# A four-layer graph network on one core: the step grid cut from 100 to 98 blocks of 32 destinations, and the dense layers' chunks from six of 512 and one of 128 to five of 512, one of 320 and one of 256

## What is computed

```python
h = relu(layernorm(x)); x = x + L0(h)   # messages relu([h[src],h[dst],ea]@mW1+mb1)@mW2, mean over dst, update, norm
h = relu(layernorm(x)); x = x + h @ W1 + b1 + segment_sum(h[src], dst) @ W2 + b2
h = relu(layernorm(x)); x = x + segment_sum(norm[:, None] * (h @ W)[src], dst) + bias
h = relu(layernorm(x)); x = x + relu(0.9 * segment_sum(h[src] * norm[:, None], dst) + 0.1 * h)
```

## Time and profile before

| what | value |
|---|---|
| device time, median of 3 runs | 948.86 us (948.36 to 949.64) |
| span of the profiled execution, first to last instruction | 946.8 us |
| PE busy | 851.2 us, 90% of the span |
| DVE, ACT, POOL busy | 67%, 54%, 55% |
| mean granted TensorE clock | 0.957 of full speed |

### The profile page before, as it was taken

How to read it: one execution, slowest core, us unless ns; L and a number is a source line. 1 busy time by engine, 2 the same in 40 slices (tenths; PEclk the granted TensorE clock), 3 DMA queues, 4 the chain that set the end, 5 groups by cost and what they waited for, 6 DMA issues and landing times.

```text
span 946.8 us, 19062 instructions
## 1 busy us (share of the span) xinstructions
PE 851.2 (90%) x6997; PEld 788.9 (83%) x6997; DVE 636.1 (67%) x1758; ACT 510.7 (54%) x1013; POOL 520.9 (55%) x496
## 2 busy tenths in 40 slices
PE   3257889889898978999989999999999999999997
PEld 2257879879898978989989999987889888888886
DVE  6528979887786877779897989968743311115664
ACT  2224757556575656768777788853353011114873
POOL 5477777777777777777777777745110000023110
PEclk9667999999898989999999999999999999999999
DMA  8752556556565666556565556656247778784500
GB/s 206 199 109 71 159 160 209 165 159 214 174 200 158 173 142 192 165 165 204 168 184 156 176 159 196 176 172 195 70 157 274 295 297 299 297 287 139 165 23 27
DMA packets 109503, 168.91 MB, mean 178 GB/s; under 512 B 14723, under 2 KB 69545, under 8 KB 109406
## 3 DMA queue, kind: packets, MB, share of 16 engines
q1 hardware_dynamic: 92062, 137.01, 44.8%
q0 software_dynamic: 13648, 28.21, 11.5%
q10 hardware_dynamic: 3696, 2.42, 0.9%
HBM read 109.15 MB, written 58.44 MB: 177 GB/s over the span
## 4 chain that ended last, share of the span: by engine, by line
PE 43%; POOL 38%; issue 13%; DMA 4%; ACT 1%; SPq 1%; DVE 1%; ACTq 0%; POOLq 0%; DVEq 0%
POOL room L769 36%; PE ps L1889 14%; PE ps L1874 14%; PE ps L1714 2%; DMA room<-p_rows,idx 2%; PE ps L1715 2%; PE ps L1728 2%; PE ps L1858 2%; PE ps L1745 2%; PE ps L1747 2%; PE ps L1650 1%; DMA w_m<-in_L_gnn_mW 1%; POOL pair L769 1%; DMA p_rows<-g 1%; ACTq L905 0%
## 5 line engine op out<-in xcount | busy, mean ns | idle before, releaser
L769 POOL DMA_INDIRECT room<-p_rows,idx x416 | 438.0, 1053 | 137.5 <-issue 125.0
L1714 PE MATMUL ps<-room,ident 128*128 128x128 f32 x832 | 178.8, 299 | 59.7 <-DMA room<-p_rows,idx 58.9
L1714 PEld LDWEIGHTS ps<-room,ident 128*128 128x128 f32 x832 | 135.5, 205 | 63.5 <-DMA room<-p_rows,idx 45.6
L1715 PE MATMUL ps<-room 128*128 128x128 f32 x832 | 170.6, 289 | 0.0
L1745 PE MATMUL ps<-room 128*128 128x200 bf16 x800 | 161.3, 253 | 0.0
L1747 PE MATMUL ps<-room 128*128 128x100 bf16 x1600 | 160.6, 208 | 0.0
L1294 DVE TENSOR_TENSOR room<-room,Wp 128x800 bf16<-128x800 bf16 x300 | 155.4, 571 | 0.0
L1747 PEld LDWEIGHTS ps<-room 128*128 128x128 bf16 x1600 | 147.9, 98 | 3.9
L1889 PE MATMUL ps<-room,h 128*128 128x256 f32 (+1 forms) x650 | 136.2, 371 | 0.0
L1715 PEld LDWEIGHTS ps<-room 128*128 128x128 f32 x832 | 136.0, 205 | 0.0
L927 ACT ACTIVATE g<-ps 128x512 f32<-128x512 f32 x104 | 62.2, 598 | 136.8 <-PE ps L1715 136.7
(11 more groups left out here) (195 smaller groups left out, 1132.1 us busy)
## 6 DMA issues: line engine op xcount, KB each, us to landing
weight_blocks<-room SPq DMA_DIRECT2D x50, 800.0 KB, 4.6
room<-weight_blocks SPq DMA_DIRECT2D x12, 3200.0 KB
room<-dst_row SPq DMA_DIRECT2D x52, 256.0 KB
room<-count_blocks SPq DMA_DIRECT2D x8, 1600.0 KB
count_blocks<-room SPq DMA_DIRECT2D x50, 200.0 KB
room<-p_rows,idx POOLq DMA_INDIRECT x416
first_c<-count_blocks SPq DMA_DIRECT2D x4, 1600.0 KB, 10.0
edge_windows<-room SPq DMA_DIRECT2D x1, 3072.0 KB
```

The costliest lines, as they stand in the source:

```text
L769: return pool.indirect_dma_start(to, None, table, bass.IndirectOffsetOnAxis(ap=at, axis=0))
L1714: pe.matmul(to, ident[:, :], G[:, n % GS, c, :], start=True, stop=False)
L1715: last = pe.matmul(to, sT[:, n % TS, 128 * c:128 * c + 128], Qr[:, n % QS, :], start=False, stop=True)
```

## The change

Destinations 3136 to 3199 exist only as padding. `STEPS` becomes (3135 + 1) / 32 = 98, so the sweep has 98 block steps (none at q = 102 and 103), and both dense matrices end at column 3136. `CHUNKS` gives each chunk's steps: five of 16, one of 10, one of 8. Chunk edges no longer fall on tile edges, so the node side has lists of its own, `SETTLED[j]`: the tiles that are complete once chunk j is; they hold 4, 4, 4, 4, 4, 2 and 3 tiles. What reads or writes sums goes by chunks (`chunk_of`, `chunk_width`), what works on nodes after them by `SETTLED`. In layer 2 chunk 5 has two halves of 5 steps and chunk 6 one of 8 (`halves_of`); there are thirteen, as before. The count bytes of layer 3's chunk 2 now wait for the last half of layer 2 (13), not the tenth, since that half fills its buffer. The store of the last chunk is two DMAs. The rest of the diff replaces `TILES` by `SETTLED` in the same way, or is the fallback.

```diff
-    STEPS = NP // 32
+    STEPS = (PAD_DST + 1) // 32
+    CHUNKS = [16] * 5 + [10, 8]
+    BEFORE = [sum(CHUNKS[:j]) for j in range(len(CHUNKS))]
+    ENDS = [32 * (b + c) // 128 for b, c in zip(BEFORE[:-1], CHUNKS)] + [NT]
+    SETTLED = [list(range(ENDS[j - 1] if j else 0, ENDS[j])) for j in range(NC)]
...
+        def chunk_of(a, j):
+            return a[:, 32 * BEFORE[j]:32 * BEFORE[j] + chunk_width(j)]
+
+        def halves_of(j):
+
+            c = CHUNKS[j]
+            return [(BEFORE[j], c)] if c <= UC // 2 else [(BEFORE[j], c // 2), (BEFORE[j] + c // 2, c - c // 2)]
...
         def chunk_steps(j):
-            return UC * j, min(UC, STEPS - UC * j)
+            return BEFORE[j], CHUNKS[j]
...
-                        sp.wait_ge(s_den[2], (11, 10, 2 * NC - 1)[j - 1])
+                        sp.wait_ge(s_den[2], (11, 2 * NC - 1, 2 * NC - 1)[j - 1])
...
-                for j, tiles in enumerate(TILES):
+                for j, tiles in enumerate(SETTLED):
                     sp.wait_ge(s_fin, r * NC + j + 1)
...
-                if u >= 0:
+                if 0 <= u < STEPS:
                     blocks(u, 0)
                 seg(q)
...
-                for half in range(2 if j < NC - 1 else 1):
-                    c = min(UC // 2, STEPS - UC * j - UC // 2 * half)
+                for half, (u0, c) in enumerate(halves_of(j)):
+                    at = 32 * (u0 - BEFORE[j])
                     pe.wait_ge(*landed(2, j, half))
...
-                        last = pe.matmul(bank(dense_bank(j))[:, 256 * half:256 * half + 32 * c], h[:, t, :],
+                        last = pe.matmul(bank(dense_bank(j))[:, at:at + 32 * c], h[:, t, :],
```

More of the change, by code:

```diff
@@ L406, in part_of, with settled_width, settled_of, settled_cols @@
             return a[:, 512 * j:512 * j + width(j)]
+        def settled_width(j):
+            return 128 * len(SETTLED[j])
+        def settled_of(a, j):
+            return a[:, SETTLED[j][0]:SETTLED[j][-1] + 1, :]
+        def settled_cols(a, j):
+            return a[:, 128 * SETTLED[j][0]:128 * SETTLED[j][-1] + 128]
+        def settled_at(t):
+            return min(j for j in range(NC) if t < ENDS[j])
+        def chunk_width(j):
+            return 32 * CHUNKS[j]
+        def chunk_of(a, j):
[3 more added lines that the diff above has]
+            return [(BEFORE[j], c)] if c <= UC // 2 else [(BEFORE[j], c // 2), (BEFORE[j] + c // 2, c - c // 2)]
         def bank_of(j):
[L409 removed]
+            return bank(j, settled_width(j)).rearrange("p (t d) -> p t d", d=D)
         hi_read = Hr[:, :, 0, :].bitcast(fp32)
@@ L433, in slot_bank, with stored_blocks @@
             return bank(2 + q % 2)[:, 256:512]
-        def stored_blocks():
-            return 16 * (STEPS // OUTS)
+        def stored_blocks(k):
+            return 16 * len([u for u in range(0, STEPS, 2) if u // 2 % (OUTS // 2) == k])
         ORDER = {1: [0, 1, 2, 3, 5, 6, 7, 4] + list(range(8, GROUPS_1)), 3: list(range(GROUPS_1))}
@@ L476, in chunk_steps @@
         def chunk_steps(j):
-            return UC * j, min(UC, STEPS - UC * j)
+            return BEFORE[j], CHUNKS[j]
         LOADS = [(1, j, 0) for j in range(1, NC)]
-        LOADS += [(2, j, half) for j in range(NC) for half in range(2)][:2 * NC - 1]
+        LOADS += [(2, j, half) for j in range(NC) for half in range(len(halves_of(j)))]
+        assert len(LOADS) == 3 * NC - 2
         LOADS += [(3, j, 0) for j in range(NC)]
@@ L606, in _ @@
                 u = q - LAG
-                if u >= 0 and u % 2 == 1:
+                if 0 <= u < STEPS and u % 2 == 1:
                     k = u // 2 % (OUTS // 2)
@@ L1134, in _ @@
                 again_sums(2)
-                pipeline((0, root(3, 1)), (1, rows(3, 1, h, ACT.Relu, x)))
+                pipeline((0, root(3, 1, SETTLED)), (1, rows(3, 1, h, ACT.Relu, x, SETTLED)))
                 again_sums(3)
-                pipeline((0, root(4, 1)), (1, scaled_rows(1)))
+                pipeline((0, root(4, 1, SETTLED)), (1, scaled_rows(1)))
                 for j in range(NC):
@@ L1542, in layer2 @@
                 pipeline((0, lambda j: add_sums(j) if r == 0 else None), (1, add_O2(r)),
-                         (1, norm(4, r, more=((DINV3, rs3, nb3), (SELF3, rs2, nb2)))))
+                         (1, norm(4, r, more=((DINV3, rs3, nb3), (SELF3, rs2, nb2)), parts=SETTLED)))
             def late_part(r, j):
                 dve.wait_ge(s_bias, r * NC + j + 1)
-                link(dve.tensor_tensor(tiles_of(x, j), tiles_of(x, j), tiles_of(h, j), ALU.add))
+                link(dve.tensor_tensor(settled_of(x, j), settled_of(x, j), settled_of(h, j), ALU.add))
             def lo_rows(j):
@@ L1561, in finish @@
                 link(last)
-                dve.scalar_tensor_tensor(tiles_of(h, j), tiles_of(own, j), 0.0, tiles_of(x, j), ALU.max, ALU.add)\
+                dve.scalar_tensor_tensor(settled_of(h, j), settled_of(own, j), 0.0, settled_of(x, j), ALU.max, ALU.add)\
                     .then_inc(s_fin, 1)
```

90 lines of the change are left out of this document (46 added, 44 removed).

## The result

| | before | changed |
|---|---|---|
| device time, median on one chip | 949.68 us (948.36 to 953.24) | 944.62 us (940.23 to 946.87) |
| ratio to the kernel before | 1 | 0.9932 [0.9908, 0.9957] |
| span of the profiled execution | 946.8 us | 942.3 us |
| mean granted TensorE clock | 0.957 | 0.958 |

What follows compares the result with a forecast made beforehand. PE was taken as the bound over most of the dense layers. Terms -1.3 - 3.42 - 2.6 - 0.4 - 3.42 + 1.5 = -9.6 us took the median from 948.86 to 939.2 us, range 936.0 to 944.4.

Steps and rivals of the forecast that it cites:

- What bounds the kernel: PE, busy without gap from about 642 to 862 us: a PE microsecond saved there is one of the run saved.
- Part 1, the sweep's end: Sweep's end with fewer block steps: 0.3 us from an earlier cast, 0.94 from earlier loads, about -1.3 us.
- With the load 9 us earlier these go, 0.94 us: Layer 1's start: PE's wait at group 5 and two slowed groups after it vanish as count loads come earlier.
- Part 2, layers 1 and 3: Chunks 5 and 6 at 320 and 256 columns, 149 and 122 ns a matmul: 13.58 for 17.00 us, -3.42 a layer.
- Part 3, layer 2: Layer 2's last chunks, 138 ns a matmul at 160 columns: 24.57 for 27.17 us, -2.6 us.
- Part 4, between layers 2 and 3: Layer 3's group 4 ready about 0.8 us sooner, PE's start about 0.35 us later: -0.4 us.
- Part 5, the end: Behind the last product, more columns, tiles and a second store DMA for ACT, PE, DVE and SP: +1.5 us.
- Even growth: Rival: matmul time in layers 1 and 3 grows evenly with columns, 170 and 150 ns; 944.1 us, chance 8%.
- the plain fp32 price: Rival: 256 columns in layers 1 and 3 cost 216 ns as in layer 2; 948.6 us, no change, chance 5%.
- 0.87 ns a column: Rival: chunks under 512 columns in layers 1 and 3 pay this, +8.0 us a layer; 962 us, chance 4%.
- That PE keeps the sweep's end: Rival: PE keeps the whole 2.9 us saved at the sweep's end, 2.6 us more; 936.6 us, chance 11%.
- The slower side: Rival: dearer columns below 512 in layers 1 and 3 make the kernel slower, sum +13.2; 962 us, chance 4%.

Runs made afterwards that it cites:

- the second execution: The changed kernel unaltered, timed again on another chip: 941.57 us, ratio 0.9911 to the kernel before.
- 98 steps alone: The changed kernel with its 98 steps but the old chunk sizes, six of 512 columns and a last one of 64: 955.58 us, ratio 1.0031.
- the zero matmuls: The changed kernel with fourteen unused bf16 matmuls of zeros on PE ahead of piece 11's `A`: 940.94 us, ratio 0.9880.
- all three: The changed kernel with layer 1's group 0 ahead of `A`, three POOL casts held for DVE steps, and group 8 before the last transposes: 938.17 us, ratio 0.9845.
- busy, group 8 early: The changed kernel with fourteen matmuls of zeros ahead of `A` and layer 1's group 8 before the last two transposes: 939.29 us, ratio 0.9856.
- busy, timed casts: The changed kernel with fourteen matmuls of zeros ahead of `A` and POOL's casts of groups 5, 6, 7 held for DVE steps: 938.13 us, ratio 0.9863.

## Why the prediction was right in sign and too large

- **What bounds the kernel** held: from chunk 2 on, PE time saved was span saved.
- **Part 1, the sweep's end, failed**: -1.3 us forecast, +2.83 measured (+3.04 in the second execution, +0.61 in "98 steps alone", which shares it). Two of its steps were right: `A` held by DVE's `add`, PE idle for some 3 us. "With the load 9 us earlier these go, 0.94 us" was right about POOL (no wait at group 5) and wrong about the sum. The step that failed is the idle time itself, which had been priced at nothing: behind it the granted clock fell to 0.50, and what follows (group 0, `U`, the chain of piece 11) came later, ACT's read of `U` by 2.90 us and `hT` by 3.09. A second step was missing: an earlier load means an earlier cast, and that cast holds steps of DVE. Against the kernel before, this is not the loss, since from `U` to `hT` both take about as long (19.62 and 19.43 us). But it keeps the loss from being had back by the clock alone: when piece 11 comes earlier, the casts fall on the steps of piece 10 (21.31 us from `U` to `hT` with the zero matmuls). With the clock kept and the casts held part 1 comes to -1.43 (40.13 for 41.56). That this lies beside the -1.3 forecast is luck: the held casts also take away a stretch that the kernel before had, 2.56 us for 0.56. The prediction had the second mechanism in its rows (DVE's step of 1.62 us "until POOL's cast [...] was over") and did not ask what an earlier cast would meet. One slip of reading changes nothing: the block rows from 621.83 to 623.27 are sixteen rows, eight pairs.
- **Part 2, layers 1 and 3**: -3.42 a layer forecast for the two chunks, -3.71 measured (147 and 119 ns for 149 and 122). 512, 384, 320 and 256 columns at 229, 175, 147 and 119 ns lie on one line of 0.43 ns a column, and 128 and 64 columns at 111 and 112 on the floor of the weight load. From chunk 2 to the start of layer 2 it is 57.02 for 60.77 us, -3.75; in layer 3, from its group 6 to the last product, 58.87 for 62.81 us, -3.94. What makes the further 0.2 in layer 3 was not looked into.
- **Part 3, layer 2**: -2.6 forecast, -2.77 measured (24.40 for 27.17; 136 ns at 160 columns, 138 forecast). The loads came in time.
- **Part 4, between layers 2 and 3**: -0.4 forecast, -0.71 measured from the end of layer 2's last half to group 6 of layer 3 (15.65 for 16.36 us). The wait of 0.77 us went; layer 3's first matmul starts 1.19 us behind layer 2, where it was 0.87 (+0.35 forecast).
- **Part 5, the end**: +1.5 forecast, +1.99 measured, of which 1.59 up to SP's last issue (3.34 for 1.75).
- Parts 2 to 5 sum to -9.18 where -8.34 was forecast; with part 1 it is -6.35 for -9.64, and the sweep's variation of 1.85 us makes that the -4.5 of the spans.
- **The rivals.** Even growth (170 and 150 ns), the plain fp32 price (216) and 0.87 ns a column (278 and 222) are all refuted by 147 and 119. By the figures of the Trainium skill ("TensorE: Matmul & The Clock Gate", section "Back-to-back issue gap") that the prediction weighed, 320 and 256 columns would have been an estimated 106 and 98 ns; the rows, 147 and 119, go against it. That PE keeps the sweep's end did not come. The slower side was sought in the columns; it lay in the sweep, where no rival stood.

## What to carry to other kernels

Work taken off PE ahead of a wait may not be free even where PE waits anyway: ask what the granted clock does behind the gap, and put other real work into it (here a group of the next layer, at no cost). A transfer that comes earlier sets free work on another engine: look what it then runs beside. And take two suspected waits away together as well as singly, since parallel chains hide each other.

## What the runs showed of the hardware

- Gaps on PE around the sweep's end and the granted clock behind them, each from a row of one of these executions: 1.00, 1.11, 1.41, 1.53 and 1.94 us left it at 1.00; 2.26, 2.47, 2.51, 2.86, 3.13, 3.23 and 3.46 us were followed by 0.50. But the length of a gap did not decide it: earlier in the sweep 3.58 us ("all three", up to 124.23) and 3.39 us ("busy, group 8 early", up to 318.73) left the clock at 1.00, while 1.84 us (the kernel before, up to 322.67) and 1.81 us ("busy, timed casts", up to 483.15) were followed by 0.50. So one execution in which the clock stays up does not show that its gap is safe.
- The loss differed: behind the gap ahead of `A`, group 0 took 4.14 to 4.63 us, and in some executions `A` or `U` were stretched too.
- In "98 steps alone" a stream of fp32r matmuls of 64 columns lost the clock with PE busy in every window; the chunk of 128 columns in the kernel before kept 1.00. The shorter last chunk was therefore slower, 7.66 us for 5.54.
- DVE steps with two operands in SBUF, 0.16 to 0.56 us alone, took up to 2.56 us beside POOL's cast of 2.32 us.
